# A ViT tower on one core: the convolution stage looks one plane ahead instead of two

## The chip, the cores and the metric

The kernel runs on one core of one Trainium2 chip. The metric is the device time of one execution in microseconds; the kernel before took 1901.03 us (median of 3 runs, 1897.28 to 1901.47). The engines are PE (TensorE), DVE (VectorE), ACT (ScalarE), POOL (GpSimd) and SP (SyncE, which issues the DMAs). Each has its own queue of instructions and waits on semaphores for the others.

## What is computed

16 images of 3 channels of 256x256 go through a normalised template correlation, then through an attention layer and a gated MLP with layer norms. Only the first stage is touched:

```python
result = dw_conv2d(image, norm_t)              # 31x31 template, one per channel
m1  = dw_conv2d(image, ones/961)               # box mean
m2  = dw_conv2d(image * image, ones/961)       # box mean of squares
std = sqrt(m2 - m1 * m1)
h   = (result / (std + eps)).mean(axis=channel)  # nan -> 0
h = layernorm(h + attention(h));  h = layernorm(h + ffn(h))
```

## The kernel before, in words

`token_stage` handles planes: a plane is one channel of a group of 4 images (`GI`); 4 groups (`GROUPS`) of 3 channels make 12 planes, n = 0 to 11. A stage behind it (attention, then the MLP) starts when all engines have left this one.

For a plane n:

- SP loads the columns (`load_xt`, L231, waits until the down sums of the plane before are done) and the patches (`load_x`, L227, waits until the plane before is split). Each has a single buffer, `xt` and `xp`.
- The two box sums are sliding sums on DVE, a scan instruction each (L422). `sum_down(n, q)` sums along one axis, for the pixels (q = 0) and their squares (q = 1, from ACT's `square`, L309). ACT's `regroup` (L318) puts the result into `down_m`, PE transposes it (`turn_sums`, L567; its first half, k = 0 to 3, is q = 0, its second half, k = 4 to 7, is q = 1), ACT's `turned` (L328) copies it from PSUM into `lines`, and DVE's `sum_across(n, q)` sums along the other axis into `box`.
- ACT's `mean_square` (L333) and DVE's `variance` (L447, L451) give the variance. ACT's `deviation` takes the root (L337), the logarithm (L339) and the exponential (L341), each with a table load. DVE's `inverse` (L456, L459, L463 or L465) refines it to 1/std and notes where it is valid.
- The patches are split into two half-precision parts (ACT's `split_hi`, L304; DVE's `split_lo`, L471), and PE's `correlate(c, n, b)` (L586) multiplies them with the template bands: 330 matmuls a plane, in four banks b = 0 to 3 of 75, 90, 90 and 75. DVE's `scale` (L483; for c > 0 also L489, for c = 2 also L492) empties a bank. `correlate(n + 1, b)` waits for `scale(n, b)`.

`planes` (L195) writes out each engine's order: `first()`, then a hardware loop over the groups whose body is three calls of `body`, then three calls for the last group. PE's loop starts at group 1, since planes 0 to 2 are written out in its `first()`.

In the body for plane n the engines work on planes n, n + 1 and n + 2. DVE does `inverse(n)`, then `split_lo(n + 1)`, and between the four `scale(n, b)` it does `sum_down(n + 2)`, `sum_across(n + 1)` and, ahead of the last two, `variance(n + 1)`. ACT does `split_hi(n + 1)`, `square(n + 2)`, all of `turned(n + 1)`, `mean_square(n + 1)`, `regroup(n + 2)` and last `deviation(n + 1)`. PE does bank 0, the first transposing half of n + 1, bank 1, the second half, banks 2 and 3. In the last bodies DVE also prepares the next stage's weights (`fold_weights`, L500) and scales the first tokens (`scale_tokens`, L511), and POOL splits the weights (L284).

Of the kernel before, what the change touches and what calls it, by code (L numbers as in the profile page):

```python
# [15 lines left out]
IMGS, CHANNELS, SIDE = 16, 3, 256  # L16
# [6 lines left out]
GROUPS = IMGS // GI  # L23
# [99 lines left out]
def token_stage(nc, sh, X, XT, TF, TPAD, H, WORDS, WEIGHTS, WQKV, NW, GQ, GK):  # L123
# [6 lines left out]
    with ExitStack() as ctx:  # L130
# [61 lines left out]
        block = ctx.enter_context(nc.Block())  # L192
        LAST = GROUPS * CHANNELS - 1

        def planes(eng, body, first, start=0):  # L195


            first()
            with eng.Fori(start, GROUPS - 1) as g:
                for c in range(CHANNELS):  # L200
                    body(g, c, g * CHANNELS + c, False)
            for c in range(CHANNELS):
                body(GROUPS - 1, c, LAST - CHANNELS + 1 + c, True)


        def after(g, c):
            return (g, c + 1) if c + 1 < CHANNELS else (g + 1, 0)

        @block.sync
        def _(sp):  # L210
            sp.dma_start(tmpl, TF).then_inc(s_tload, 16)
            sp.dma_start(xt[:], XT[0, 0].rearrange("p (b w) -> p b w", b=2)).then_inc(s_xt, 16)
            sp.dma_start(xp[:], X[0, 0]).then_inc(s_xp, 16)

            for k in range(2):
                sp.wait_ge(s_tdve, 6 + k)
                sp.dma_start(TPAD[k], tpad[k]).then_inc(s_tpad, 16)
            sp.wait_ge(s_tpad, 32)

            def load_bands(c):  # L220
                size = (RI * PR - 1) * TCOLS + CJ * PC
                for k, w in enumerate((w_hi, w_lo)):
                    src = bass.AP(tensor=TPAD.tensor, offset=(k * CHANNELS + c) * TROWS * TCOLS,
                                  ap=[[TCOLS, PR], [1, PC], [1, size]])
                    sp.dma_start(w[:, c, 0:size], src).then_inc(s_band[c], 16)

            def load_x(g, c, n):  # L227
                sp.wait_ge(s_lo, n + 1)
                sp.dma_start(xp[:], X[g, c]).then_inc(s_xp, 16)

            def load_xt(g, c, n):  # L231
                sp.wait_ge(s_down, n * 4 + 1)
                sp.dma_start(xt[:], XT[g, c].rearrange("p (b w) -> p b w", b=2)).then_inc(s_xt, 16)

            def first():
                load_bands(0)
                load_xt(0, 1, 1)
                load_x(0, 1, 1)
                load_bands(1)
                load_bands(2)  # L240
                load_xt(0, 2, 2)

            def body(g, c, n, last):
                if not (last and c >= 1):
                    load_x(*after(*after(g, c)), n + 2)
                if not last:
                    load_xt(g + 1, c, n + CHANNELS)
                if c < 2:
                    size = P // GROUPS // 2
                    rows = bass.ds(g * (2 * size) + c * size, size)  # L250
                    sp.dma_start(WORDS[rows], WEIGHTS[rows]).then_inc(s_copies, 16)
                if c == 2:
                    sp.wait_ge(s_result, g * 4 + 8)
                    sp.dma_start(H[g], total.rearrange("p a c -> p (a c)")).then_inc(s_store, 16)
                if last and c == 1:
                    sp.wait_ge(s_down, LAST * 4 + 5)
                    for half in range(2):
                        sp.dma_start(staged[half], WQKV[:, :, half * WH:half * WH + WH]).then_inc(sh.s_wload[half], 16)
                    for dst, src in ((sh.norm_w, NW), (sh.gq, GQ), (sh.gamma, GK)):
                        sp.dma_start(dst[:], src).then_inc(sh.s_small, 16)  # L260
                    sp.wait_ge(s_box, 2 * LAST + 4)
                    sp.wait_ge(s_store, 32)
                    sp.dma_start(sh.hn, H[0].rearrange("p (a c) -> p a c", a=PR)).then_inc(sh.s_hn, 16)

            planes(sp, body, first)
            sp.wait_ge(s_copies, 16 * 2 * GROUPS)

# [28 lines left out]
        def _(act):  # L296
# [9 lines left out]
            def square(n):  # L306
                act.wait_ge(s_xt, n * 16 + 16)
                act.wait_ge(s_down, n * 4 + 1)
                act.activation(xt_sq[:], xt[:], ACT.Square).then_inc(s_sq, 1)  # L309
# [37 lines left out]
            def first():  # L347
                square(0)
                split_hi(0, 0)
                regroup(0, 0)  # L350
                act.wait_ge(s_const, 7)
                turned(0, 0)
                regroup(0, 1)
                square(1)
                mean_square(0)
                turned(0, 1)
                regroup(1, 0)
                act.wait_ge(s_tpad, 32)
                deviation(0)
                regroup(1, 1)  # L360

            def body(g, c, n, last):
                if not (last and c == 2):
                    split_hi((c + 1) % CHANNELS, n + 1)
                if not (last and c >= 1):
                    square(n + 2)
                if not (last and c == 2):
                    turned(n + 1, 0)
                    turned(n + 1, 1)
                    mean_square(n + 1)  # L370
                if not (last and c >= 1):
                    regroup(n + 2, 0)
                    regroup(n + 2, 1)
                if not (last and c == 2):
                    deviation(n + 1)
                if last and c == 2:
                    for k, (half, f) in enumerate(WPARTS):
                        act.wait_ge(sh.s_wprep, k + 1)
                        act.activation(sh.w_hi[:, f, half * WH:half * WH + WH], staged[half][:, f], ACT.Copy)\  # L379
                           .then_inc(sh.s_whi, 1)  # L380
                    act.wait_ge(sh.s_hn, 16)
                    for a in range(PR):
                        ins = act.activation(sh.squares[:, a * D:(a + 1) * D], sh.hn[:, a], ACT.Square,
                                             accum_out=sh.ss[:, a:a + 1])
                    ins.then_inc(sh.s_hsum, 1)
            planes(act, body, first)

        @block.vector
        def _(dve):
# [124 lines left out]
            def first():  # L514
                sum_down(0, 0)
                split_lo(0, 0)
                sum_down(0, 1)
                sum_across(0, 0)
                sum_down(1, 0)
                sum_across(0, 1)  # L520
                variance(0)
                sum_down(1, 1)
                dve.wait_ge(s_tpad, 32)

            def body(g, c, n, last):
                more, more_down = not (last and c == 2), not (last and c >= 1)
                dve.wait_ge(s_part, n * 4 + 4)
                inverse(g, c, n)
                if last and c == 2:
                    fold_weights()  # L530
                if more:
                    split_lo((c + 1) % CHANNELS, n + 1)
                if more_down:
                    sum_down(n + 2, 0)
                scale(g, c, n, 0)
                if more:
                    sum_across(n + 1, 0)
                if more_down:
                    sum_down(n + 2, 1)
                scale(g, c, n, 1)  # L540
                if last and c == 2:
                    scale_tokens()
                if more:
                    sum_across(n + 1, 1)
                    variance(n + 1)
                scale(g, c, n, 2)
                scale(g, c, n, 3)

            planes(dve, body, first)
# [2 lines left out]
        def _(pe):  # L552
# [35 lines left out]
                ins.then_inc(s_conv, 1)  # L588

            def first():  # L590
                turn_sums(0, range(4))
                correlate(0, 0, 0)
                turn_sums(0, range(4, 8))
                correlate(0, 0, 1)
                correlate(0, 0, 2)
                turn_sums(1, range(4))
                correlate(0, 0, 3)
                turn_sums(1, range(4, 8))
                for c in range(1, CHANNELS):
                    body(0, c, c, False)  # L600

            def body(g, c, n, last):
                correlate(c, n, 0)
                if not (last and c == 2):
                    turn_sums(n + 1, range(4))
                correlate(c, n, 1)
                if not (last and c == 2):
                    turn_sums(n + 1, range(4, 8))
                correlate(c, n, 2)
                correlate(c, n, 3)  # L610

            planes(pe, body, first, 1)

# [991 lines left out]
```

## Time and profile before

| | |
|---|---|
| median of 3 runs | 1901.03 us |
| the profiled execution | 1905.45 us |
| its span | 1903.6 us |
| mean granted clock of TensorE | 0.973 |
| PE busy | 1789.2 us (94%) |
| DVE busy | 1109.4 us (58%) |
| ACT busy | 870.3 us (46%) |
| the three correlation matmul groups (L586) | 355.7, 356.6 and 355.2 us busy, 1320 each |

The convolution stage is the first part of the span: the last matmul of L586 starts at 553.03 us. Matmuls overlap one another, so the busy time of a group is longer than its share of the engine; the distance between starts is what counts. The granted clock is a share of full speed: 1.00 is 2.4 GHz, 0.50 is 1.2 GHz.

### The profile page before, as it was taken

What the parts mean: (1) busy time and instruction counts of PE and PEld (TensorE: products, weight loads), DVE (VectorE), ACT (ScalarE), POOL (GpSimd) and SP (SyncE); (2) the same over time, 40 slices, a digit from 0 to 9 for tenths busy, and PEclk for the clock granted to TensorE, in tenths of its full rate; (3) what the DMA queues carried; (4) which work ended last, traced back from release to release, by engine and by line L of the source; (5) the groups of instructions that cost most, each with busy time, mean ns of one, the idle gap of its engine ahead of it and who ended that gap; (6) DMA issues with size and microseconds to landing.
All of it is one profiled execution on the core that took longest, in us unless ns stands there. A gap on an engine that the chain in (4) does not pass through costs nothing. (4 is left out here: it accounts for less than half of the span.)

```text
span 1903.6 us, 31322 instructions
## 1 busy us (share of the span) xinstructions
PE 1789.2 (94%) x11640; PEld 1554.9 (82%) x11640; DVE 1109.4 (58%) x1964; ACT 870.3 (46%) x1073; POOL 424.4 (22%) x516
## 2 busy tenths in 40 slices
PE   5988999999988999998999999899999999999998
PEld 4888998988976877787787788778888888888886
DVE  8788888888766565676557575343241423414142
ACT  4655544555525674676477477322221222222221
POOL 2000000000020221222122122143433434434342
PEclk9989999999988999999999999899999999999999
DMA  5321222224101000200200010350000000000000
GB/s 171 119 81 73 81 106 74 81 81 147 54 34 60 24 16 10 91 23 17 83 24 20 26 54 24 108 191 23 1 23 0 22 0 22 22 0 23 1 12 13
DMA packets 26344, 96.79 MB, mean 51 GB/s; under 512 B 3033, under 2 KB 11353, under 8 KB 20962
## 3 DMA queue, kind: packets, MB, share of 16 engines
q1 hardware_dynamic: 26210, 94.96, 14.6%
q8 instruction: 90, 1.47, 0.3%
q14 instruction: 44, 0.36, 0.1%
HBM read 82.33 MB, written 24.15 MB: 56 GB/s over the span
## 5 line engine op out<-in xcount | busy, mean ns | idle before, releaser
L586 PE MATMUL conv<-w_hi,x_hi 128*128 128x368 f16 (+5 forms) x1320 | 355.7, 279 | 7.9 <-issue 6.0
L586 PE MATMUL conv<-w_lo,x_hi 128*128 128x368 f16 (+5 forms) x1320 | 356.6, 279 | 0.0
L586 PE MATMUL conv<-w_hi,x_lo 128*128 128x368 f16 (+5 forms) x1320 | 355.2, 279 | 0.0
L1354 ACT ACTIVATE raw_c<-ring,sh 128x512 f32<-128x512 f32 x128 | 87.5, 689 | 334.4 <-PE ring L1457 334.3
L864 POOL TENSOR_SCALAR_AFFINE_SELECT probs<-probs 128x256 f32<-128x256 f32 x256 | 123.9, 508 | 435.2 <-ACT probs L940 435.2
L1142 PE MATMUL mixed<-v,probs 128*128 128x65 f32 x1536 | 198.7, 280 | 15.6 <-DVE o L1024 12.0
L1142 PEld LDWEIGHTS mixed<-v,probs 128*128 128x128 f32 x1536 | 182.4, 193 | 32.0 <-issue 17.5
L1366 DVE CAST ha_hi<-raw_c 128x512 fp32r<-128x512 f32 x128 | 90.6, 708 | 201.0 <-ACT raw_c L1354 198.8
L1313 POOL TENSOR_TENSOR ha_lo<-raw_c,ha_hi 128x512 fp32r<-128x512 f32 x128 | 165.3, 1291 | 187.8 <-DVE ha_hi L1366 187.8
L586 PEld LDWEIGHTS conv<-w_hi,x_hi 128*128 128x128 f16 x1320 | 193.2, 146 | 16.9 <-issue 8.5
L1457 PE MATMUL ring<-ha_hi,wh 128*128 128x512 f32 x512 | 199.6, 390 | 0.9 <-POOL ha_lo L1313 0.9
L586 PEld LDWEIGHTS conv<-w_lo,x_hi 128*128 128x128 f16 x1320 | 192.9, 146 | 8.4 <-issue 0.2
L586 PEld LDWEIGHTS conv<-w_hi,x_lo 128*128 128x128 f16 x1320 | 192.9, 146 | 8.3 <-issue 0.3
L1457 PE MATMUL ring<-hb_lo,wh 128*128 128x512 f32 x512 | 199.5, 390 | 0.0
L1457 PE MATMUL ring<-ha_lo,wh 128*128 128x512 f32 x512 | 199.5, 390 | 0.0
L1457 PE MATMUL ring<-hb_hi,wh 128*128 128x512 f32 x512 | 199.4, 389 | 0.0
L937 ACT ACTIVATE probs<-sim 128x768 f32<-128x768 f32 x128 | 103.8, 811 | 97.6 <-PE sim L1128 96.0
L1366 DVE CAST hb_hi<-raw_c 128x512 fp32r<-128x512 f32 x64 | 35.8, 559 | 185.3 <-ACT raw_c L1354 185.2
L1128 PE MATMUL sim<-qt,kt 64*128 64x256 f32 (+1 forms) x1024 | 120.2, 354 | 3.2 <-DVE kt L1014 2.8
L422 DVE TENSOR_TENSOR_SCAN box<-lines 128x271 f32<-128x271 f32 x192 | 120.2, 699 | 4.4 <-ACT lines L328 4.4
L1128 PEld LDWEIGHTS sim<-qt,kt 64*128 64x128 f32 x1024 | 90.0, 189 | 39.7 <-issue 32.9
L284 POOL TENSOR_TENSOR wqkv_lo<-xt,wqkv_hi 128x1024 fp32r<-128x1024 f32 x2 | 4.8, 2388 | 518.2 <-ACT wqkv_hi L379 518.2
(147 smaller groups left out, 3491.0 us busy)
## 6 DMA issues: line engine op xcount, KB each, us to landing
xt<-x_columns_in SPq DMA_DIRECT2D x12, 1163.0 KB, 5.6
xp<-x_patches_in SPq DMA_DIRECT2D x12, 1152.0 KB, 5.2
hidden_words<-hidden_weights_in SPq DMA_DIRECT2D x8, 1408.0 KB, 9.0
words<-hidden_words SPq DMA_DIRECT2D x32, 352.0 KB, 3.0
wh<-hidden_words SPq DMA_DIRECT2D x8, 1024.0 KB, 10.0
tokens<-planes SPq DMA_DIRECT2D x4, 1024.0 KB, 4.3
lines<-tokens SPq DMA_DIRECT2D x4, 1024.0 KB, 5.6
h<-tokens SPq DMA_DIRECT2D x4, 1024.0 KB, 6.9
```

What stands on the lines that cost most here:

```text
L284: pool.tensor_tensor(sh.w_lo[:, f, cols], staged[half][:, f], sh.w_hi[:, f, cols].bitcast(F32), ALU.subtract).then_inc(sh.s_wlo, 1)
L422: return dve.tensor_tensor_scan(out, line[:, TH:TH + SCAN], line[:, 0:SCAN], 0.0, ALU.add, ALU.subtract)
L586: ins = pe.matmul(out, xs[:, c, RI - 1 - i:RI - 1 - i + NR, :, x].rearrange("p r g -> p (r g)"), w, start=(t == 0), stop=(t == len(terms) ...
L864: ins = pool.affine_select(out=diag, in_=diag, compare_op=ALU.is_ge, fill=0.0, base=0, pattern=[[0, 2], [1, P]], channel_multiplier=-1)
L937: act.activation(probs[:, n % 4], sim[:, n % 2, :, 0:3 * P], ACT.Tanh, scale=1.0 / CLAMP).then_inc(s_tanh, 1)
L1128: ins = pe.matmul(sim[:, n % 2, m, 2 * P * jb:2 * P * jb + P * (2 - jb)], kt[rows, img % 2, hd, P * jb:P * jb + P], qt[rows, img % 2, hd, ...
L1142: ins = pe.matmul(out, probs[:, n % 4, m, at:at + P], v[:, img % 2, jb, 2 * (hd // 2) + m], start=(jb == 0), stop=(jb == ib), skip_group_c ...
L1313: pool.tensor_tensor(dst[1][:, u % KH], raw[:, u % 4], dst[0][:, u % KH].bitcast(F32), ALU.subtract).then_inc(s_lo, 1)
L1354: act.activation(raw[:, u % 4], bank, ACT.Gelu, scale=scale[:, m:m + 1]).then_inc(s_gelu, 1)
L1366: dve.tensor_copy(dst[0][:, u % KH], raw[:, u % 4]).then_inc(s_hi, 1)
L1457: ins = pe.matmul(bank, a, b, start=start, stop=False, skip_group_check=True)
```

## The change

All engines work in the body of plane n on planes n and n + 1 only. DVE finishes plane n's box sums there (`sum_across(n, 1)`, `variance(n)`), then does both `sum_down(n + 1)`, then `inverse(n)`, `split_lo(n + 1)`, three scalings, `sum_across(n + 1, 0)` and the fourth. ACT finishes `turned(n, 1)` and `mean_square(n)`, splits and squares plane n + 1, does `deviation(n)` and then `regroup(n + 1)` and `turned(n + 1, 0)`. PE does banks 0 to 2, the first transposing half of n + 1, bank 3, the second half. SP loads the columns of plane n + 2 instead of n + 3, ahead of the patches. `first()` is shorter on every engine, and PE's loop begins at group 0 like the others.

```diff
-        def planes(eng, body, first, start=0):
+        def planes(eng, body, first):
             first()
-            with eng.Fori(start, GROUPS - 1) as g:
+            with eng.Fori(0, GROUPS - 1) as g:
...
                 load_bands(1)
                 load_bands(2)
-                load_xt(0, 2, 2)
 
             def body(g, c, n, last):
                 if not (last and c >= 1):
+                    load_xt(*after(*after(g, c)), n + 2)
                     load_x(*after(*after(g, c)), n + 2)
-                if not last:
-                    load_xt(g + 1, c, n + CHANNELS)
...
                 act.wait_ge(s_const, 7)
                 turned(0, 0)
                 regroup(0, 1)
-                square(1)
-                mean_square(0)
-                turned(0, 1)
-                regroup(1, 0)
                 act.wait_ge(s_tpad, 32)
-                deviation(0)
-                regroup(1, 1)
 
             def body(g, c, n, last):
-                if not (last and c == 2):
+                more = not (last and c == 2)
+                turned(n, 1)
+                mean_square(n)
+                if more:
                     split_hi((c + 1) % CHANNELS, n + 1)
-                if not (last and c >= 1):
-                    square(n + 2)
-                if not (last and c == 2):
+                    square(n + 1)
+                deviation(n)
+                if more:
+                    regroup(n + 1, 0)
+                    regroup(n + 1, 1)
                     turned(n + 1, 0)
-                    turned(n + 1, 1)
-                    mean_square(n + 1)
-                if not (last and c >= 1):
-                    regroup(n + 2, 0)
-                    regroup(n + 2, 1)
-                if not (last and c == 2):
-                    deviation(n + 1)
...
                 sum_across(0, 0)
-                sum_down(1, 0)
-                sum_across(0, 1)
-                variance(0)
-                sum_down(1, 1)
                 dve.wait_ge(s_tpad, 32)
 
             def body(g, c, n, last):
-                more, more_down = not (last and c == 2), not (last and c >= 1)
+                more = not (last and c == 2)
+                sum_across(n, 1)
+                variance(n)
+                if more:
+                    sum_down(n + 1, 0)
+                    sum_down(n + 1, 1)
+                else:
+                    fold_weights()
                 dve.wait_ge(s_part, n * 4 + 4)
                 inverse(g, c, n)
-                if last and c == 2:
-                    fold_weights()
                 if more:
                     split_lo((c + 1) % CHANNELS, n + 1)
-                if more_down:
-                    sum_down(n + 2, 0)
-                scale(g, c, n, 0)
+                for b in range(3):
+                    scale(g, c, n, b)
                 if more:
                     sum_across(n + 1, 0)
-                if more_down:
-                    sum_down(n + 2, 1)
-                scale(g, c, n, 1)
-                if last and c == 2:
+                else:
                     scale_tokens()
-                if more:
-                    sum_across(n + 1, 1)
-                    variance(n + 1)
-                scale(g, c, n, 2)
                 scale(g, c, n, 3)
...
             def first():
-                turn_sums(0, range(4))
-                correlate(0, 0, 0)
-                turn_sums(0, range(4, 8))
-                correlate(0, 0, 1)
-                correlate(0, 0, 2)
-                turn_sums(1, range(4))
-                correlate(0, 0, 3)
-                turn_sums(1, range(4, 8))
-                for c in range(1, CHANNELS):
-                    body(0, c, c, False)
+                turn_sums(0, range(8))
 
             def body(g, c, n, last):
-                correlate(c, n, 0)
-                if not (last and c == 2):
+                more = not (last and c == 2)
+                for b in range(3):
+                    correlate(c, n, b)
+                if more:
                     turn_sums(n + 1, range(4))
-                correlate(c, n, 1)
-                if not (last and c == 2):
+                correlate(c, n, 3)
+                if more:
                     turn_sums(n + 1, range(4, 8))
-                correlate(c, n, 2)
-                correlate(c, n, 3)
-
-            planes(pe, body, first, 1)
+
+            planes(pe, body, first)
```

## Rows read from the trace of the kernel before

**Rows 1.** Busy time by stretch: us, then each engine, then clock and DMA.

```profile
60.00:520.00 460.00, 433.18 (x3746) 409.77 (x3745) 392.23 (x485) 248.56 (x224) 0.00 (x0) 0.97 0.24 89
...
1400.00:1600.00 200.00, 199.71 (x959) 167.70 (x959) 78.72 (x136) 49.38 (x69) 83.02 (x72) 1.00 0.05 16
```

**Rows 2.** Waits, 60 to 520 us: who waited for whom, total, times, longest.

```profile
DVE std L456 <- ACT guess L341: 60.5, 10, 7.4
PE turn L567 <- ACT lines L328: 24.8, 7, 10.1
```

**Rows 3.** Timeline of PE: start, us, what; idle before and its releaser.

```profile
16.83 3.42 PE L567 MATMUL turn<-ident,down_m 128*128 128x128 f32 x16 [16.83 <-ACT down_m L318]
...
26.22 0.38 PE L586 MATMUL conv<-w_hi,x_hi 128*128 128x217 f16 x1 [5.97 <-issue]
...
68.95 0.60 PE L567 MATMUL turn<-ident,down_m 128*128 128x128 f32 x4
...
221.66 1.93 PE L567 MATMUL turn<-ident,down_m 128*128 128x128 f32 x16
223.42 0.21 PE L586 MATMUL conv<-w_hi,x_hi 128*128 128x105 f16 x1
...
262.55 1.92 PE L567 MATMUL turn<-ident,down_m 128*128 128x128 f32 x16
...
553.03 0.26 PE L586 MATMUL conv<-w_hi,x_lo 128*128 128x217 f16 x1
```

**Rows 4.** PE's timeline between planes 5 and 6, and the stretch after.

```profile
296.51 0.26 PE L586 MATMUL conv<-w_hi,x_lo 128*128 128x217 f16 x1
298.72 0.32 PE L586 MATMUL conv<-w_hi,x_hi 128*128 128x217 f16 x1 [1.95 <-DVE planes L483]
...
298.70:302.70 4.00, 3.98 (x22) 3.03 (x23) 3.97 (x7) 1.33 (x2) 0.00 (x0) 0.63 0.84 297
```

**Rows 5.** Timeline of DVE, the body of plane 5 (c = 2).

```profile
271.48 2.29 DVE L456 SCALAR_TENSOR_TENSOR std<-std,guess 128x2048 f32<-128x2048 f32 x1 [5.96 <-ACT guess L341]
...
278.21 2.55 DVE L471 TENSOR_TENSOR x_lo<-xp,x_hi 128x2304 f16<-128x2304 f32 x1
280.68 5.01 DVE L422 TENSOR_TENSOR_SCAN down<-xt 128x271 f32<-128x271 f32 x8
285.60 0.67 DVE L483 SCALAR_TENSOR_TENSOR planes<-conv,planes 128x512 f32<-128x512 f32 x1
...
287.74 5.01 DVE L422 TENSOR_TENSOR_SCAN box<-lines 128x271 f32<-128x271 f32 x8
...
299.69 5.01 DVE L422 TENSOR_TENSOR_SCAN box<-lines 128x271 f32<-128x271 f32 x8
...
308.31 0.68 DVE L483 SCALAR_TENSOR_TENSOR planes<-conv,planes 128x512 f32<-128x512 f32 x1
```

**Rows 6.** Timeline of ACT: the start, one copy, and the body of plane 5.

```profile
23.05 1.06 ACT L318 ACTIVATE down_m<-down 128x1024 f32<-128x1024 f32 x1 [1.22 <-DVE down L422]
...
69.67 0.60 ACT L328 ACTIVATE lines<-turn 128x512 f32<-128x512 f32 x1 [6.33 <-PE turn L567]
...
273.30 2.13 ACT L309 ACTIVATE xt_sq<-xt 128x2326 f32<-128x2326 f32 x1
...
294.71 4.04 ACT L318 ACTIVATE down_m<-down 128x1024 f32<-128x1024 f32 x4
...
308.43 1.92 ACT L337 ACTIVATE std<-std 128x2048 f32<-128x2048 f32 x1 [8.38 <-DVE std L451]
...
314.98 1.92 ACT L341 ACTIVATE guess<-guess 128x2048 f32<-128x2048 f32 x1
```

**Rows 7.** DMA issues on the page: KB each, median us to landing.

```profile
xp<-x_patches_in SPq DMA_DIRECT2D x12, 1152.0 KB, 5.2
```

**Rows 8.** Timeline of DVE at the stage's end.

```profile
541.16 8.60 DVE L511 TENSOR_SCALAR lines<-lines,rms 128x256 f32<-128x256 f32 x8 [1.90 <-POOL rms L291]
...
553.33 0.69 DVE L483 SCALAR_TENSOR_TENSOR planes<-conv,planes 128x512 f32<-128x512 f32 x1 [1.51 <-PE conv L586]
```

## The prediction

> **What bounds the kernel now.** I began with the engine shares by stretch. In the long middle of the convolution stage PE is busy 433.18 of 460.00 us at a mean clock of 0.97, DVE 392.23 [rows 1]. So PE is the fullest engine, but not a full one: some engine keeps it waiting. The table of waits says who. PE's own waits are at the transposes (L567), for ACT's copies (L328): 24.8 us in 7 waits. Behind them DVE waits 60.5 us for ACT's exponential (L341) before the first operation of `inverse` [rows 2].
>
> The two go together. Before the change DVE's plane is a circle: `variance(n+1)`, two scalings, then `inverse(n+1)`, which needs ACT's root, logarithm and exponential of that very variance. The reader is to see in the DVE timeline that nothing of substance stands between variance and inverse: after the variance stand only the scalings from 308.31 on, two times 2.14 us, to 312.6 [rows 5], and ACT's chain from that variance runs from 308.43 to 314.98 + 1.92 = 316.9 [rows 6]. So DVE and ACT take turns, and PE, whose transposes sit behind ACT's copies, which stand behind the same deviation in ACT's queue, waits in turn.
>
> How much does PE lose? A plane without a pause, from one transposing half to the same half of the next plane, takes 262.55 - 221.66 = 40.89 us; a half itself takes 223.42 - 221.66 = 1.76 [rows 3]. The 330 correlation matmuls are thus 40.89 - 3.52 = 37.37. From the first correlation at 26.22 to the last at 553.03 + 0.10 are 526.9 us [rows 3]. In it lie 12 planes and 23 halves (the first half of plane 0 is earlier): 12 x 37.37 + 23 x 1.76 = 488.9. PE loses 38.0 us in the stage, most of it idle, the rest at the lower clock after pauses.
>
> **The change, part by part.** Take t = 0 where PE starts the second transposing half of plane n, with its third plane of a group (c = 2, the dearest on DVE) as the case.
>
> PE: halves at t = 0 to 1.76; correlate 0, 1, 2 end at about 1.76 + 37.37 x 255 / 330 = 30.6; first half of n + 1 to 32.4; correlate 3 to 40.9, which is the next t = 0.
>
> DVE: ACT's first copy begins 69.67 - 68.95 = 0.72 after the transposes [rows 3, 6], takes 0.6, so `sum_across(n, 1)` starts at 1.35. It and variance take 308.31 - 299.69 = 8.62 [rows 5], to 10.0. Now come the two `sum_down` of the next plane, 2 x (285.60 - 280.68) = 9.84, to 19.8. `inverse` needs ACT: from the variance's end to the exponential's end are 8.5 us (308.4 to 316.9) [rows 5, 6], so it may run from 18.6, and the two `sum_down` have covered that: the stall (60.5 us in 10 waits [rows 2]) goes. `inverse` 278.21 - 271.48 = 6.73 to 26.5, `split_lo` 2.47 to 29.0, two scalings at 287.74 - 285.60 = 2.14 to 33.3, the third to 35.4, `sum_across(n + 1, 0)` 4.92 to 40.3, the fourth scaling after correlate 3, to 43.0 [rows 5]. That is 2.1 past the next t = 0, where 1.35 is the earliest DVE could go on anyway; planes with c = 0 or 1 have shorter scalings (the sums and `valid` are missing) and win it back.
>
> ACT: copies to 2.8, mean square, `split_hi`, `square` at about 2.13 each to 9.2, then 1.3 for the root's table (the wait of 8.38 us before 308.43 begins 1.3 after 294.71 + 4.04) to 10.5; the variance is there at 10.0, so ACT is 0.5 late, against 1.2 spare at `inverse`, the chain to 19.1, four regroups 4.04 to 23.1, then the copies of the first half [rows 6]. What is queued behind ACT's wait for the variance is the regroups, and PE waits for those only at 30.6: 7.5 us to spare. PE's other needs are `split_lo` (29.0) and the first scaling (31.1) at 42.7: over 11 us to spare. What comes late next is therefore PE itself.
>
> SP: the load of the columns now waits for `sum_down(n + 1)` at 19.8 and is read 27.8 later; that of the patches goes at 29.0 and is read some 16 later. Such a load lands in 5.2 us [rows 7]. The copy of the hidden weights is now behind the patches, at 29 instead of after the columns; nothing in the stage reads it. The token store waits for the fourth scaling, and behind it in SP's queue is only a load that could not start before t = 19.8 of the next plane. All this at nothing; if a landing took three times as long, the patches' spare time would be gone.
>
> The start: `turn_sums(0, range(8))` now puts the second half ahead of the first correlation. It waits for ACT's regroup, 23.05 + 1.06 = 24.1 [rows 6], and runs at the low clock, 3.4 us as the first half did at 16.83 [rows 3]; the correlation starts at 27.5 instead of 26.22, with a quarter us lost to the low clock until the faster one is granted (before, the correlation itself bought it with 2 us). Full-speed start: 27.75.
>
> The loop: there is one more thing in PE's idle time. Between the matmuls at 296.51 and 298.72 PE stands for 2.1 us, and the granted clock is then 0.63 over 4.0 us [rows 4], 1.5 us lost: 3.6. The row puts it down to DVE's scaling L483. But what this matmul waits for (bank 0 free again) was done at 285.60 + 0.67 [rows 5]; in the code this is where PE's loop jumps back from plane 5 to plane 6. Before, PE's loop runs from 1 to 2, one jump; after, from 0 to 2, two. So this loss doesn't go, it doubles: 7.2 us. Bounds for each: 0 (if the row's label is right) and 3.6. I take 3.6, from the only such place there is. The jumps of DVE and ACT stand in time to spare.
>
> A rule speaks against the change here. The Trainium skill (Runtime: NRT & Kernel Launch, Instruction fetch mechanics) says that instructions are fetched ahead only in sequence and that a taken branch to a target outside the small window stalls until it is fetched. By the row's label the stage would be 7.2 us shorter than by that rule; that PE stands between two matmuls whose operands are ready agrees with the rule.
>
> The tail: before, the scaling of tokens takes 8.60 us from 541.16 on, and the last scaling starts at 553.33, with the last matmul's end [rows 8]. After, the weights' preparation falls into the wait for `inverse`, and the tokens' scaling follows the third scaling at 30.6 + 2.1 = 32.7 of its plane. If it takes 8.60 again it ends at 41.3, and the last matmul ends at 39.1: between 0 and 2.2 us late. I take 0, since eight operations of 128x256 in 8.60 us are slow beside one of 128x2048 in 2.29 [rows 5]: most of the 8.60 is a disturbance from elsewhere that need not last.
>
> The sum: 27.75 + 12 x 37.37 + 22 x 1.76 = 514.9; with two jumps 522.1, against 553.1. That is 31.0 us less. Everything behind the stage starts at its end and moves with it. The profiled execution took 1905.45 us (span 1903.6), so it would be 1874.4; the median of the runs shown, 1901.03, lies 4.4 lower and becomes 1870.0.
>
> **The rivals.**
> (a) The jumps cost nothing: a further 7.2, 1862.8. For it the label on the row; against it the code. 0.10.
> (b) A part of PE's waits stays, because the lookahead has one plane less: DVE's c = 2 plane has 41.1 us of work against PE's 40.9, and its jump adds to it. Without the spare time found above that costs 43.0 - 40.9 = 2.1 at each of 4 planes, and with 2.2 of tail 10.6 us: 1880.6. With one ACT wait of the old size (60.5 / 10 = 6) left, 1887. 0.17.
> (c) Slower: the clock falls where PE never rests. Each hundredth of clock in 487 us costs 4.9 us; from 31.0 / 4.9 = 6.3 hundredths the gain is gone, and at 0.90 the time is 1870 + 54 = 1924. Against it: over 1400 to 1600 PE is busy 199.71 of 200.00 us at 1.00 [rows 1]. 0.06.
> (d) The order has changed but PE waits as long, at another place: 1901. Against it the spare 7.5 us. 0.04.
>
> **How the numbers follow.** The forecast, 1866 to 1876, has 0.63. With (a) and the nearer two thirds of (b), 1861 to 1885 holds a good 0.8. About 0.2% (4 us) is what can be told from no change. Faster: 0.63 + 0.10 + 0.17 = 0.90. Same: 0.04. Slower: 0.06.
>
> **What would show it.** PE's plane at 40.9 us throughout; no wait of L567 for L328 except at the start; no wait of L456 for L341, DVE instead waiting at L483 for PE and at L422 for ACT's copies; two pauses of 2 us in PE, each where the loop jumps after the second half of planes 3 and 6, each followed by a low clock; the last matmul at 522. Wrong would be: a PE wait at the transposes of every plane (b, d), a clock under 1.00 without a pause before it (c), no pause at the jumps (a), or a last scaling well after the last matmul.

## The result

The changed kernel takes 1874.24 us (median of 4 runs, 1873.01 to 1875.93), the kernel before in the same comparison 1899.79 us. The ratio is 0.9859, 95% interval 0.9843 to 0.9875: faster by 25.6 us or 1.4%. The profiled execution took 1875.0 us with a span of 1873.3, against 1905.45 and 1903.6.

**Busy time by stretch** of after answers to [rows 1]:

```profile
60.00:520.00 460.00, 455.91 (x4029) 433.16 (x4027) 410.51 (x501) 258.63 (x244) 15.52 (x6) 1.00 0.23 85
1400.00:1600.00 200.00, 198.17 (x937) 165.80 (x936) 59.82 (x109) 46.13 (x65) 78.29 (x66) 1.00 0.04 11
```

PE went from 433.18 to 455.91 us of 460, and its clock from 0.97 to 1.00. It is now the bound. **The waits** of after, 20 to 530 us, answer to [rows 2]:

```profile
DVE planes L473 <- PE conv L569: 36.6, 15, 4.5
ACT std L335 <- DVE std L441: 7.1, 7, 4.4
DVE std L446 <- ACT guess L339: 5.6, 1, 5.6
...
PE turn L550 <- ACT down_m L316: 3.9, 1, 3.9
```

The direction has turned. DVE used to wait 60.5 us for ACT's exponential; one such wait is left, in the last plane, where only the preparation of the next stage's weights, some 3 us, stands in the place of the down sums. Instead DVE waits 36.6 us at its scalings for PE. PE's transposes (L550) wait once, at the start, and no more from 60 us on, where they had waited 24.8 us. **PE's timeline** of after answers to [rows 3] and [rows 4]:

```profile
24.16 3.68 PE L550 MATMUL turn<-ident,down_m 128*128 128x128 f32 x16 [3.91 <-ACT down_m L316]
27.63 0.39 PE L569 MATMUL conv<-w_hi,x_hi 128*128 128x217 f16 x1
...
67.93 1.91 PE L550 MATMUL turn<-ident,down_m 128*128 128x128 f32 x16
...
98.15 1.92 PE L550 MATMUL turn<-ident,down_m 128*128 128x128 f32 x16
...
108.77 1.91 PE L550 MATMUL turn<-ident,down_m 128*128 128x128 f32 x16
...
149.61 1.91 PE L550 MATMUL turn<-ident,down_m 128*128 128x128 f32 x16
153.38 0.31 PE L569 MATMUL conv<-w_hi,x_hi 128*128 128x217 f16 x1 [1.85 <-issue]
...
277.75 0.31 PE L569 MATMUL conv<-w_hi,x_hi 128*128 128x217 f16 x1 [1.68 <-issue]
...
519.18 0.26 PE L569 MATMUL conv<-w_hi,x_lo 128*128 128x217 f16 x1
```

From one second transposing half to the next a plane is 108.77 - 67.93 = 40.84 us, and the next 40.84 again; the row at 98.15 is a first half. Two pauses are left, both right after a second transposing half, both now put down to "issue", that is, to no other engine. **DVE's body** for plane 2 (c = 2) answers to [rows 5]:

```profile
110.31 5.01 DVE L412 TENSOR_TENSOR_SCAN box<-lines 128x271 f32<-128x271 f32 x8
115.35 2.29 DVE L437 SCALAR_TENSOR_TENSOR var<-box,var 128x2048 f32<-128x2048 f32 x1
...
128.76 2.26 DVE L446 SCALAR_TENSOR_TENSOR std<-std,guess 128x2048 f32<-128x2048 f32 x1
...
149.81 0.69 DVE L473 SCALAR_TENSOR_TENSOR planes<-conv,planes 128x512 f32<-128x512 f32 x1 [0.44 <-PE conv L569]
```

Between variance and `inverse` (L446) now stand the down sums, and L446 begins without a wait at 128.76, while ACT's exponential had ended at 127.5. **ACT** answers to [rows 6]:

```profile
119.04 1.93 ACT L335 ACTIVATE std<-std 128x2048 f32<-128x2048 f32 x1 [0.31 <-DVE std L441]
...
125.61 1.93 ACT L339 ACTIVATE guess<-guess 128x2048 f32<-128x2048 f32 x1
127.44 3.91 ACT L316 ACTIVATE down_m<-down 128x1024 f32<-128x1024 f32 x4
139.72 1.58 ACT L326 ACTIVATE lines<-turn 128x512 f32<-128x512 f32 x3 [8.37 <-PE turn L550]
```

The regroups begin 127.44 - 108.77 = 18.7 us after t = 0; their first pair is done about 2 us later, and PE asks for it at 98.15 - 67.93 = 30.2, so there are 9.5 us to spare. DVE has less: its fourth scaling (149.81) waits only 0.44 us for PE. **The tail** answers to [rows 8], DVE's timeline first:

```profile
501.31 4.39 DVE L449 SCALAR_TENSOR_TENSOR planes<-std,guess 128x2048 f32<-128x2048 f32 x1
...
512.99 2.77 DVE L482 TENSOR_TENSOR planes<-planes,valid 128x512 f32<-128x512 f32 x1
...
519.19 2.18 DVE L501 TENSOR_SCALAR lines<-lines,rms 128x256 f32<-128x256 f32 x8
521.29 0.68 DVE L473 SCALAR_TENSOR_TENSOR planes<-conv,planes 128x512 f32<-128x512 f32 x1
```

and POOL's:

```profile
499.88 3.66 POOL L282 TENSOR_TENSOR wqkv_lo<-xt,wqkv_hi 128x1024 fp32r<-128x1024 f32 x1 [486.35 <-ACT wqkv_hi L369]
...
509.69 2.72 POOL L282 TENSOR_TENSOR wqkv_lo<-xt,wqkv_hi 128x1024 fp32r<-128x1024 f32 x1
512.37 5.62 POOL L282 TENSOR_TENSOR wqkv_lo<-xt_sq,wqkv_hi 128x1024 fp32r<-128x1024 f32 x2
```

The last scaling starts 2.1 us after the last matmul (519.18), where before it was 0.3.

### The profile page after: what moved, and what is told of

The parts are those of the page before. It is cut to its first block and busy times, and to the rows that moved or that the text cites. A ratio compares the mean times of both kernels' runs of the same rounds, so it can differ in the third digit from the quotient of the medians.

```text
span 1873.3 us, 31348 instructions
## 1 busy us (share of the span) xinstructions
PE 1781.0 (95%) x11640; PEld 1548.6 (83%) x11640; DVE 1104.9 (59%) x1964; ACT 873.9 (47%) x1077; POOL 429.0 (23%) x516
## 5 line engine op out<-in xcount | busy, mean ns | idle before, releaser
L1340 DVE CAST ha_hi<-raw_c 128x512 fp32r<-128x512 f32 x128 | 86.3, 674 | 201.0 <-ACT raw_c L1328 198.8
L326 ACT ACTIVATE lines<-turn 128x512 f32<-128x512 f32 x96 | 50.0, 606 | 172.1 <-PE turn L550 172.1
```

What stands on the lines that cost most here:

```text
L326: act.activation(dst, turn[:, k % 4], ACT.Copy).then_inc(s_across, 1)
L1340: dve.tensor_copy(dst[0][:, u % KH], raw[:, u % 4]).then_inc(s_hi, 1)
```

## The experiments

### The changed kernel again, as the yardstick

> The changed kernel once more, unaltered, as the yardstick for the others of this job. The theory (PE is the bound and pauses only where its loop jumps back) expects about 1874 us, 25 us under the kernel before, two pauses of 1.7 to 1.9 us in PE, after the second transposing half of planes 3 and 6, and a PE plane of 40.8 us everywhere else. Whether the clock falls after these pauses is open: the forecast said 1.5 us lost each time, the first trace shows none.

1874.43 us (ratio 0.9864, 0.9845 to 0.9883). The pauses were 1.83 and 2.19 us. After the second the clock fell, in the stretch behind it:

```profile
277.70:281.70 4.00, 3.98 (x20) 3.12 (x21) 3.88 (x7) 4.00 (x3) 0.00 (x0) 0.57 0.50 199
```

and the last matmul came at 520.87 instead of 519.18. So the clock's part of the price of a pause is there in one execution and not in another.

### PE's loop written out, in the changed kernel

```diff
-            planes(pe, body, first)
+            first()
+            for n in range(LAST + 1):
+                body(n // CHANNELS, n % CHANNELS, n, n // CHANNELS == GROUPS - 1)
```

> The changed kernel with PE's hardware loop written out: twelve bodies in a row, no jump. Theory (the pauses are the jump): both pauses go, the last correlation matmul ends 3.5 us earlier, 1870.7 us. Rival (the pauses are a wait for another engine, DVE or the token store, that falls at the same place): the pauses stay and the time is that of the changed kernel, 1874.

1870.23 us (ratio 0.984, 0.9819 to 0.986), 4.2 us under the unaltered changed kernel in the same comparison. No pause is left in PE's timeline between 27.63 and the last matmul:

```profile
515.08 0.26 PE L569 MATMUL conv<-w_hi,x_lo 128*128 128x217 f16 x1
```

That is 4.1 us earlier than in after, and from 60 to 515 us PE is busy for 455.00 of 455.00. With nothing else altered the pauses went, so they are the loop's jump back. This agrees with the Trainium skill (Runtime: NRT & Kernel Launch, Instruction fetch mechanics), by which a taken branch to a target outside the small window of fetched instructions stalls until the target is fetched. What the engine does in the pause no row shows.

### PE's loop written out, in the kernel before

The same edit with `range(CHANNELS, LAST + 1)`.

> The kernel before with PE's hardware loop written out. Its trace shows one pause in the middle of the correlations, 2.1 us at 298.7 us, put down to DVE's scaling. Theory (it is the loop's jump): this pause goes and 2 to 4 us with it if PE is the bound there; but DVE and ACT set the pace of the kernel before, so PE only waits longer at the next transposes, and the time changes by 0 to 2 us, 1898 to 1900. Rival (a wait for DVE): the pause stays.

The pause that the trace had put down to DVE's L483 is gone, so it too was the jump. The waits at the transposes grew to 27.1 us in 7 (24.8 before), and the last matmul came at 551.91, 1.1 us earlier. DVE and ACT set the pace, and what PE saved it waited for later. The runs took 1906.82 us, ratio 1.003 (1.001 to 1.005), slower than expected by some 7 us, although the profiled execution of it (1904.5) was no longer than that of before. Why the unprofiled runs are slower I cannot say from these rows.

### Two planes ahead, but with the cover

```diff
-                if more_down:
-                    sum_down(n + 2, 0)
                 scale(g, c, n, 0)
...
-                if more_down:
-                    sum_down(n + 2, 1)
                 scale(g, c, n, 1)
...
                     sum_across(n + 1, 1)
                     variance(n + 1)
+                if more_down:
+                    sum_down(n + 2, 0)
+                    sum_down(n + 2, 1)
                 scale(g, c, n, 2)
```

and on ACT `deviation(n + 1)` ahead of `regroup(n + 2)`.

> The kernel before, still two planes ahead and with its own PE order, but with the two down sums of plane n + 2 put between the variance of n + 1 and the last two scalings on DVE, and the regroups behind the deviation on ACT. Theory (the gain is that DVE has 9.8 us of work of its own while ACT makes the deviation; how far ahead it looks does not matter): DVE's waits for ACT's exponential go, PE runs at 40.9 us a plane, 1872 to 1882 us (the written-out first planes may keep a pause). Rival (the gain comes from looking one plane ahead, with the transposes late in the plane): at most a few us under the kernel before, 1893 to 1900.

(ACT has to change too, since the down sums that `regroup(n + 2)` waits for now come after the variance.) 1881.1 us (ratio 0.9911, 0.9884 to 0.9938): faster than before by 0.9%, against 1.4% for the change. In its waits from 60 to 520 us L456 no longer waits for L341, PE's plane is 225.49 - 184.61 = 40.88 us by the starts of two transposing halves, and PE has two pauses:

```profile
DVE planes L483 <- PE conv L585: 38.0, 14, 7.5
...
PE turn L566 <- ACT down_m L318: 9.7, 1, 9.7
...
PE conv L585 <- DVE planes L483: 1.8, 1, 1.8
```

The 1.8 is the jump. The 9.7 is in the written-out first planes, whose order I left as it was. Its last matmul is at 530.42, 22.6 us before that of before (553.03) and 11.2 behind that of after. So two thirds of the gain in the stage (22.6 of 33.9 us) come from covering ACT's chain, without the shorter lookahead. The rest goes with the shorter start, which has no pause of 9.7 us; that is read from these rows, as no run takes that pause away by itself.

### One plane ahead, without the cover

```diff
-                if more:
-                    sum_down(n + 1, 0)
-                    sum_down(n + 1, 1)
-                else:
+                if not more:
                     fold_weights()
                 dve.wait_ge(s_part, n * 4 + 4)
                 inverse(g, c, n)
                 if more:
                     split_lo((c + 1) % CHANNELS, n + 1)
+                    sum_down(n + 1, 0)
+                    sum_down(n + 1, 1)
```

> The changed kernel, one plane ahead, but with DVE's two down sums moved from before `inverse` to behind `split_lo`, so that nothing stands between the variance and `inverse`. Theory (the gain is the cover of ACT's 8.6 us): DVE waits 8.5 us for ACT in each plane and becomes the bound, with planes of about 42.5 (c = 0), 46.4 and 49.6 us (c = 2) and the handshake with PE on top: PE waits at the transposes, 60 to 100 us over the changed kernel, 1935 to 1975 us, slower than before. Rival (the order of PE's transposes makes the gain): within 10 us of 1874.

1939.21 us, ratio 1.02 (1.0166 to 1.0233). The waits:

```profile
DVE std L446 <- ACT guess L339: 94.8, 11, 8.6
...
PE turn L549 <- ACT down_m L316: 45.2, 12, 5.9
```

The stall of 8.6 us is back in 11 planes and is larger than it was in before (60.5 us in 10), where two scalings covered part of it. PE's 12 waits are the one at the start and one in each of 11 planes. In this order a lookahead of one plane is thus worse than two; it wins by what stands in the gap.

### Four and twelve us more on ACT in each plane

```diff
                 deviation(n)
                 if more:
+                    for i in range(6):
+                        act.wait_ge(s_idle, n * 6 + i + 1)
+                        act.activation(idle[:], idle[:], ACT.Copy).then_inc(s_idle, 1)
                     regroup(n + 1, 0)
```

The second run has 18 in place of 6. `idle` is a tile of its own, 128x512, which POOL clears once at the start.

> The changed kernel with six small copies (0.6 to 0.7 us each, 4 us a plane) put on ACT between the deviation and the regroups; they add work and take nothing away. Theory (ACT's regroup has some 7.5 us to spare by the forecast, 9.7 in the trace of after, before PE waits for it): no change, 1874 us, no wait of the transposes. Rival (a lookahead of one plane is tight, every delay of ACT reaches PE): 11 planes x 4 = 44 us more.

> The same with eighteen copies, 12 us a plane. Theory: beyond the 9.7 us to spare PE waits some 2.6 us at the first transposing half of each of 11 planes, 29 us, and up to 20 us more if the clock falls after each such pause: 1903 to 1923 us. Rival (tight lookahead): 11 x 12 = 130 us more.

With 3.97 us more a plane: 1871.46 us (ratio 0.9838, 0.9806 to 0.9871), no wait of the transposes after the start, last matmul 518.53, so nothing lost. With 11.97 us: 1910.09 us (1.0032, 1.0008 to 1.0057). Its waits and one of them in the timeline:

```profile
PE turn L556 <- ACT down_m L319: 26.4, 11, 3.7
...
105.57 2.69 PE L556 MATMUL turn<-ident,down_m 128*128 128x128 f32 x16 [2.10 <-ACT down_m L319]
```

The longest of the 11, 3.7 us, is the wait at the start, which every run of the changed kernel has. The other 10, 22.7 us in all, are 1.65 to 3.13 us long and 2.3 on average, against 12.0 - 9.5 = 2.5 from the spare time read above. The eleventh plane, the one behind the first jump, has none. The last matmul is at 557.30, 38 us later than in after: 23 of it are these waits, and about 15 the clock, 0.97 on average over the 497 us from 60 to 557, where it was 1.00 in after. The spare time is real, and it ends about where it was read.

### The next stage's weights earlier

On top of the written-out loop: DVE's `fold_weights` before the last scaling of plane 10, ACT's rounding of the weights before the last deviation, POOL's first subtraction as soon as the last variance is done, and its root of the tokens' norm after all four subtractions instead of after the first.

> The changed kernel with PE's loop written out, and with the next stage's weights prepared earlier: DVE multiplies them by the norm weights before the last scaling of plane 10, where it waits 3.2 us for PE, ACT rounds them before the last deviation, and POOL subtracts while DVE waits for that deviation, so that POOL's passes no longer run beside DVE's last scalings. Theory (the last scaling starts 2.0 us after the last matmul because POOL's passes slow DVE's): it starts within 0.2 us of it, 2 us under the written-out kernel (1870.2), about 1868 us. Rival (the lateness is the tokens' scaling itself, wherever POOL is): no change from 1870.

> The fastest variant once more (PE's loop written out, the next stage's weights prepared earlier). Its first profile had a stretch of 45 us in the attention stage, from 1147 us on, with the granted clock at 0.50 while PE was busy throughout. Theory (this is chance of that execution and no effect of the edit, which ends at 518 us): the clock there is near 1 again, the span is about 1863 us, and the median stays at 1864 to 1868 us. Rival (the edit shifts the attention stage into a pattern that loses the clock): the stretch at 0.50 comes back.

1864.15 us (ratio 0.9801, 0.977 to 0.9832), and 1866.62 (0.9816, 0.98 to 0.9833) the second time: the lowest medians of all, though the intervals overlap with that of the written-out loop alone. The last scaling follows the last matmul (514.41) by 0.3 us:

```profile
497.37 2.29 DVE L452 SCALAR_TENSOR_TENSOR planes<-std,guess 128x2048 f32<-128x2048 f32 x1
...
503.42 0.69 DVE L485 TENSOR_TENSOR planes<-planes,valid 128x512 f32<-128x512 f32 x1
...
514.71 0.69 DVE L476 SCALAR_TENSOR_TENSOR planes<-conv,planes 128x512 f32<-128x512 f32 x1 [4.38 <-PE conv L571]
```

DVE even waits 4.4 us for PE there. Its operations that had been slow are back to 2.29 us (L452, which is L449 in after) and 0.69 (L485, which is L482). The next stage's first matmul came at 518.03, 2.4 us earlier than with the loop alone (520.45). The run moved work of three engines at once, so that it was POOL is read from what stood beside what: in after, the passes of 2.16 to 2.77 us begin within POOL's subtractions from 509.69 to 517.99, with ACT idle, and here, where the subtractions end at 495.2, only the first operation of `inverse` still overlaps them, and takes 3.09 instead of 2.3. So POOL's passes beside them had made the 2 us. The scalings that read PSUM (L473) took 0.68 to 0.69 us beside the same subtractions.

### The kernel before again

> The kernel before once more, unaltered. Its profiled execution was 5.7 us longer than the median of its runs, that of the changed kernel 0.8 us longer than its own. If the convolution stage of before varies from execution to execution (a pause that sometimes costs the clock, sometimes not), the last correlation matmul lies some us away from 553.1 us; if the later stages vary, it lies within 1 us of it and the rest of the span differs from the 1347 us behind it.

1901.09 us. Its last matmul came at 554.16, 1.1 us later than in the first profile, and the next stage began at 557.78, so 1902.7 - 557.8 = 1344.9 us were left, against 1903.6 - 556.65 = 1347.0. In these two executions the stage differs by about 1 us.

## Why the prediction was right, point by point

**What bounds the kernel.** Right: DVE and ACT took turns over the deviation, with PE waiting behind them. Taking the cover away (no work of DVE's own while ACT makes the deviation) costs 65 us, and giving it to the old order brings 22.6 us in the stage.

**The order in the plane.** Forecast for c = 2: variance to the down sums at 10.0, `inverse` at 19.8, fourth scaling at 40.9. Measured from t = 108.77: 10.15 (118.9), 19.99 and 41.0. The plane 40.89 forecast, 40.84 measured. ACT's spare time at the regroups was given as 7.5 us, since I counted to the end of all four; PE waits only for the first pair, and it is 9.5.

**The start.** The correlation starts at 27.63 (forecast 27.5). The quarter of a microsecond for the low clock was worked out from no row and was too little: with the loop written out the clock was 0.50 to 29.6 and 0.88 over the next microsecond, which is about 1.1 us lost. Planes 0.05 us shorter than forecast, twelve times, made up for most of it. Without jumps the last matmul was to end at 514.9; with the loop written out it ends at 515.2.

**The jumps.** Two pauses, at the places given, the label of the row (L483) being wrong as argued. The term was mis-sized: 3.6 us each, 7.2 together. The pauses measured 1.85 and 1.68, with the clock at 1.00 behind both, and writing the loop out moved the last matmul by 4.1. The one example had fallen together with a fall of the clock (1.5 us of the 3.6), and I took it as the rule. Over eight profiles with a loop in PE the clock fell after 4 of 13 such pauses, each 1.7 to 2.3 us long. So the last matmul came at 519.3 instead of 522.1.

**The tail.** Taken as 0 with 2.2 as the other end; 1.8 us were lost, near that end. The reasoning missed where the disturbance would go: the tokens' scaling did become fast (2.18 us for eight), but POOL's passes, which had made it slow, were now beside `inverse` and the scalings, and slowed those instead (L449 at 4.39 against 2.29 undisturbed, L482 at 2.77 against 0.69). A disturbance had been moved, not removed.

**The sum.** 2.8 us too pessimistic at the last matmul, 1.8 too optimistic at the tail: the next stage's first matmul moved from 556.65 to 524.61, by 32.0 us, 31.0 forecast. Behind it the rest of the span was 1.7 us longer, so the profiled execution, forecast at 1874.4, took 1875.0. That it came so near is in part luck, since these errors offset each other. For the median the forecast took over the 4.4 us by which the profiled execution of before lay above the median of its runs, and nothing supported that it would hold for the changed kernel: in before again it was 3.3, in after 0.8. So the median is 1874.2 against 1870.0, near the upper end of the range, and the gain between medians is 25.6, not the 32 of the stage.

The rest of the span, where nothing was changed, over all twelve profiles:

| profiled execution | next stage's first matmul | rest of the span |
|---|---|---|
| one ahead, uncovered | 588.47 | 1346.1 |
| 12 us more on ACT | 562.66 | 1344.9 |
| before, before again | 556.65, 557.78 | 1347.0, 1344.9 |
| before, loop written out | 555.52 | 1347.2 |
| two ahead, covered | 534.03 | 1343.9 |
| after, after again | 524.61, 526.25 | 1348.7, 1352.7 |
| 4 us more on ACT | 523.95 | 1349.1 |
| after, loop written out | 520.45 | 1344.5 |
| weights earlier, twice | 518.03, 518.02 | 1359.6, 1349.2 |

The six profiles that arrive at 534 us or later need 1344 to 1347 us there; of the six that arrive earlier, five need 1349 to 1360, and one 1344.5. It is not the changed code itself, since the first two rows have it too. It looks as if an earlier arrival costs the later stages some microseconds, but the one exception and the spread leave it open, and no run shows a cause.

**The rivals.** (a) The jumps cost nothing: wrong, 4.1 us when they are gone. (b) Waits left by the shorter lookahead: none at the transposes; of its terms only the tail's came, 1.8 of 2.2 us. (c) The clock fell where PE never rests: no, it was 1.00 over 460 us. (d) Waits as long elsewhere: none.

## What to carry to other kernels

Look in the circle of engines that sets the pace for a place where one engine hands over and has nothing of its own until the answer is back, and move independent work exactly there; here, how many planes ahead the schedule looks mattered less than what stands in that gap. Read for each consumer when it asks and when its input is ready: the difference is what later additions may cost, and here it held to a few tenths of a microsecond (waits of 2.3 us on average where 2.5 were read). Work moved earlier takes its disturbance along: ask what will stand beside it in its new place.

## What the runs showed of the hardware

At each jump back in PE's loop of 990 correlation matmuls a turn PE paused 1.68 to 2.26 us, in 13 of 13 jumps. The trace may put such a pause down to another engine: in before the releaser that it names had been done for 12 us.

After such pauses the granted clock sometimes falls: it was 0.57 over the next 4 us after 2.19 us of pause in one execution (after again), 1.00 after 1.85 us in another (after), and 1.00 after 2.25 us in a third (4 us more on ACT).

In one execution of the fastest variant (weights earlier) the clock stayed low in the attention stage with PE busy throughout:

```profile
1150.00:1170.00 20.00, 20.00 (x95) 17.53 (x95) 5.32 (x14) 7.82 (x10) 3.06 (x8) 0.50 0.50 183
```

In its second profile the same stretch was at 0.79, with PE busy 15.85 of the 20 us, and the span was 10.4 us shorter. So two profiles of one kernel can differ by 10 us in a stage that nobody touched.
